# Masked attention with LayerNorm on one core: transposes and broadcast one slot later, the finish behind the mask, and work moved from VectorE to ScalarE and GpSimd

## The reference, cut to what matters

```python
scores = einsum('nd,md->nm', x, ks)                      # 8192 x 8192, d = 128, float32
scores = leaky_relu(scores, negative_slope=0.2)
scores = where(adj > 0, scores, NEG_BIG)                 # adj: int32, 8192 x 8192
attn = softmax(scores, axis=1)
y = x + einsum('nm,md->nd', attn, ks)
out = (y - mean(y)) / sqrt(var(y) + 1e-5)                # LayerNorm over d
```

## Time and profile before

| | us |
|---|---|
| median of three runs (1758.53 to 1759.35) | 1758.76 |
| the profiled execution's own time | 1757.06 |
| its span, first to last instruction | 1755.0 |
| TensorE matmul busy | 1554.2 (89%) |
| VectorE busy | 1547.7 (88%) |
| ScalarE busy | 1441.9 (82%) |
| GpSimd busy | 1408.3 (80%) |

### The profile page before, as it was taken

How to read it: one execution, slowest core, us unless ns; L and a number is a source line. 1 busy time by engine, 2 the same in 40 slices (tenths; PEclk the granted TensorE clock), 3 DMA queues, 4 the chain that set the end, 5 groups by cost and what they waited for, 6 DMA issues and landing times. The chain is left out here.

```text
span 1755.0 us, 42403 instructions
## 1 busy us (share of the span) xinstructions
PE 1554.2 (89%) x16576; PEld 1446.4 (82%) x16576; DVE 1547.7 (88%) x1855; ACT 1441.9 (82%) x1810; POOL 1408.3 (80%) x1167
## 2 busy tenths in 40 slices
PE   2689999999999999999999999999999999999985
PEld 1488888988888988888988888888888888888885
DVE  7998989998999989899989998999898999989971
ACT  4588878888888988888989887888887888888885
POOL 0488878888888978788978887988887888878898
PEclk9899999999999999999999999999999999999999
DMA  9654445554544444445445445444444544444510
GB/s 356 232 194 151 170 159 175 178 172 159 176 163 179 166 171 173 159 171 178 168 163 178 161 171 175 174 155 175 170 164 173 175 164 169 174 164 164 176 55 7
DMA packets 67799, 296.34 MB, mean 169 GB/s; under 512 B 6160, under 2 KB 32784, under 8 KB 34832
## 3 DMA queue, kind: packets, MB, share of 16 engines
q1 hardware_dynamic: 67600, 293.63, 47.4%
HBM read 289.41 MB, written 4.19 MB: 167 GB/s over the span
## 5 line engine op out<-in xcount | busy, mean ns | idle before, releaser
L280 POOL TENSOR_TENSOR ring<-ring,floor 128x768 f32<-128x768 f32 (+1 forms) x512 | 797.5, 1558 | 100.9 <-ACT floor L374 100.9
L351 ACT ACTIVATE scores<-scores,shrink 128x1024 f32<-128x1024 f32 x512 | 553.2, 1081 | 267.3 <-PE scores L579 264.4
L479 DVE SCALAR_TENSOR_TENSOR ring<-adj_sb,scores 128x1024 f32<-128x1024 int32 x512 | 622.1, 1215 | 144.7 <-ACT scores L351 142.0
L611 PE MATMUL weighted<-k_rows,ring 128*128 128x129 f32 x4096 | 547.8, 277 | 74.3 <-DVE y L534 74.3
L577 PE MATMUL scores<-xt_hi,kt_hi 128*128 128x256 f16 x2048 | 566.1, 276 | 48.0 <-DVE xt_lo L444 29.8
L284 POOL TENSOR_TENSOR pt_lo<-ring,pt_hi 128x512 f16<-128x512 f32 x512 | 594.4, 1162 | 13.1 <-ACT pt_hi L363 13.1
L492 DVE TENSOR_TENSOR running<-ring,running 128x1024 f32<-128x1024 f32 x480 | 585.6, 1220 | 0.0
L357 ACT ACTIVATE ring<-ring,lift 128x1024 f32<-128x1024 f32 x512 | 583.9, 1140 | 1.3 <-DVE ring L513 0.7
L611 PEld LDWEIGHTS weighted<-k_rows,ring 128*128 128x128 f32 x4096 | 501.0, 192 | 87.1 <-issue 80.5
L579 PE MATMUL scores<-xt_hi,kt_lo 128*128 128x256 f16 x2048 | 566.5, 277 | 0.0
L578 PE MATMUL scores<-xt_lo,kt_hi 128*128 128x256 f16 x2048 | 566.2, 276 | 0.0
(11 more groups left out here) (50 smaller groups left out, 409.6 us busy)
## 6 DMA issues: line engine op xcount, KB each, us to landing
adj_sb<-in_adj SPq DMA_DIRECT2D x256, 1024.0 KB, 4.9
ring<-in_ks_t SPq DMA_DIRECT2D x8, 512.0 KB, 6.8
ring<-in_x_t SPq DMA_DIRECT2D x8, 512.0 KB, 13.1
xt_raw<-in_x_t SPq DMA_DIRECT2D x32, 128.0 KB, 4.8
x_row<-in_x SPq DMA_DIRECT2D x32, 128.0 KB, 4.9
out<-normed SPq DMA_DIRECT2D x32, 128.0 KB, 5.2
k_rows<-in_ks SPq DMA_DIRECT2D x16, 128.0 KB, 3.1
ring<-in_ks SPq DMA_DIRECT2D x1, 2048.0 KB, 9.3
```

Source lines behind the costliest of these rows:

```text
L280: nc.gpsimd.tensor_tensor(here, here, below, ALU.subtract).then_inc(gap_ready, 1)
L479: nc.vector.scalar_tensor_tensor(ring[:, g % RING, :, :], adj_sb[:, n % ADJS, half * QUAD:(half + 1) * QUAD, :], 0.0, scores[:, g % 2, :, ...
L611: nc.tensor.matmul(weighted[:, j * LANES:(j + 1) * LANES], ring[:, g % RING, t, j * P:(j + 1) * P], k_rows[:, q, t, 0:LANES], start=(q == ...
```

## The change

- `turn` is at delay 18 and stands, on TensorE, behind the scores of its slot and ahead of `weigh` (before: delay 17, at the slot's end). `spread` is at delay 19, and `lowest` stays at 17.
- `finish` is at delay 38 and stands on VectorE behind the slot's mask (before: 39, at the slot's head). `mean`, `squares_of`, `deviation`, `normalise` and the store follow one slot earlier, too. `mean` and `deviation` stand at the end of GpSimd's slot, and `low_part` ahead of `gap`.
- The copy of a block's first group into `running` is on ScalarE (`first`, delay 2, behind `bend`).
- The low parts of x and of four eighths of the keys are made on GpSimd, each by two instructions (scale in place, subtract) in place of one.
- In the last 16 groups VectorE takes three tiles of the `gap` and GpSimd one.
- VectorE's gap waits for the copy `floor` of its own block at all groups, and the first masks no longer wait for the keys' low parts, but for those whose ring places still hold the raw keys (8 to 15).

```diff
-    AT_TURN, AT_SPREAD = 17, 18
-    AT_FINISH = LAST + AT_WEIGH + 1
+    AT_LOWEST, AT_TURN, AT_SPREAD = 17, 18, 19
+    AT_FIRST = 2
+    AT_FINISH = LAST + AT_WEIGH
...
-            return 1 + g % 2
+            return 3 if g >= ALL - GROUPS else 1 + g % 2
...
+            def split_x(b):
+                pool.wait_ge(xt_hi_ready, b + 1)
+                wait(pool, scores_ready, GROUPS * (b - 1))
+                here = xt_raw[:, b % 2, :]
+                nc.gpsimd.tensor_scalar(here, here, scale_x, 1.0, ALU.mult, ALU.mult).then_inc(xt_scaled_ready, 1)
+                pool.wait_ge(xt_scaled_ready, b)
+                pool.wait_ge(xt_lo_ready, b)
+                nc.gpsimd.tensor_tensor(xt_lo[:, b % 2, :], here, xt_hi[:, b % 2, :], ALU.subtract)\
+                    .then_inc(xt_lo_ready, 1)
...
+            for c in range(EARLY, STEPS):
+                low_ks_t(c)
+            split_x(1)
             part_rows()
             for s in SLOTS:
+                g = group(s, AT_PART)
+                if g is not None:
+                    low_part(g)
+                g = group(s, AT_GAP)
+                if g is not None:
+                    gap(g)
                 b = whole(s, AT_FINISH + 1)
                 if b is not None:
                     mean(b)
                 b = whole(s, AT_FINISH + 2)
                 if b is not None:
                     deviation(b)
-                g = group(s, AT_GAP)
-                if g is not None:
-                    gap(g)
-                g = group(s, AT_PART)
-                if g is not None:
-                    low_part(g)
+                b = whole(s, -5)
+                if b is not None and b > 1:
+                    split_x(b)
...
+            def first(g):
+                act.wait_ge(masked_ready, g + 1)
+                wait(act, low_ready, g // GROUPS)
+                wait(act, running_ready, g)
+                nc.scalar.activation(running[:, :, :], ring[:, g % RING, :, :], ACT.Copy).then_inc(running_ready, 1)
...
-                if g < RING:
-                    dve.wait_ge(kt_lo_ready, min(STEPS, max(1, g - 7)))
+                if 8 <= g < 16:
+                    dve.wait_ge(kt_lo_ready, g - 7)
...
-            for c in range(EARLY, STEPS):
-                split_ks_t(c)
             for s in SLOTS:
+                g = group(s, 0)
+                if g is not None:
+                    mask(g)
                 b = whole(s, AT_FINISH)
                 if b is not None:
                     finish(b)
-                g = group(s, 0)
-                if g is not None:
-                    mask(g)
-                b = whole(s, AT_SPREAD - 1)
+                b = whole(s, AT_LOWEST)
                 if b is not None:
                     lowest(b)
```

More of the change, by code:

```diff
@@ L139, in adj_attention_layernorm @@
         kt_lo_ready = sem("kt_lo_ready")
+        kt_scaled_ready = sem("kt_scaled_ready")
         xt_hi_ready = sem("xt_hi_ready")
+        xt_scaled_ready = sem("xt_scaled_ready")
         xt_lo_ready = sem("xt_lo_ready")
@@ L257, in _, with low_ks_t @@
                                                bass.bass_isa.ReduceOp.max).then_inc(mag_all_ready, 1)
+            def low_ks_t(c):
+                cols = slice(c * STEP, (c + 1) * STEP)
+                pool.wait_ge(kt_hi_ready, c + 1)
+                nc.gpsimd.tensor_scalar(ks_t_raw[:, cols], ks_t_raw[:, cols], scale_k, 1.0, ALU.mult, ALU.mult)\
+                    .then_inc(kt_scaled_ready, 1)
+                pool.wait_ge(kt_scaled_ready, c - EARLY + 1)
+                pool.wait_ge(kt_lo_ready, c)
+                nc.gpsimd.tensor_tensor(kt_lo[:, cols], ks_t_raw[:, cols], kt_hi[:, cols], ALU.subtract)\
+                    .then_inc(kt_lo_ready, 1)
+            def split_x(b):
[7 more added lines that the diff above has]
+                    .then_inc(xt_lo_ready, 1)
             def part_rows():
@@ L411, in _ @@
                     spread(b)
+                b = whole(s, AT_FIRST)
+                if b is not None:
+                    first(b * GROUPS)
                 b = whole(s, -6)
-                if b is not None and b > 0:
+                if b is not None and b > 1:
                     split_x(b)
@@ L486, in least @@
                 here = ring[:, g % RING, :, :]
-                if g % GROUPS == 0:
-                    wait(dve, low_ready, g // GROUPS)
-                    nc.vector.tensor_copy(running[:, :, :], here).then_inc(running_ready, 1)
-                else:
-                    dve.wait_ge(running_ready, g)
-                    nc.vector.tensor_tensor(running[:, :, :], here, running[:, :, :], ALU.min)\
-                        .then_inc(running_ready, 1)
+                dve.wait_ge(running_ready, g)
+                nc.vector.tensor_tensor(running[:, :, :], here, running[:, :, :], ALU.min).then_inc(running_ready, 1)
             def columns(b):
@@ L501, in gap @@
             def gap(g):
-                b, j = divmod(g, GROUPS)
+                b = g // GROUPS
                 tiles = dve_tiles(g)
-                dve.wait_ge(spread_ready, b + 1)
-                if j == LAST and b + 1 < BLOCKS:
-                    dve.wait_ge(floor_ready, b + 2)
-                else:
-                    dve.wait_ge(floor_ready, b + 1)
+                dve.wait_ge(floor_ready, b + 1)
                 dve.wait_ge(running_ready, g + 1)
@@ L553, in _ @@
                 g = group(s, 1)
-                if g is not None:
+                if g is not None and g % GROUPS:
                     least(g)
@@ L557, in _ @@
                         columns(g // GROUPS)
-                b = whole(s, -5)
-                if b is not None and b > 0:
-                    split_x(b)
         @block.tensor
@@ L593, in spread @@
                 wait(pe, floor_ready, b)
-                wait(pe, dve_gap_ready, GROUPS * b - 1)
+                wait(pe, dve_gap_ready, GROUPS * b)
                 for j in range(SIDES):
@@ L634, in _ @@
                     score(g)
+                b = whole(s, AT_TURN)
+                if b is not None:
+                    turn(b)
                 b = whole(s, AT_SPREAD)
@@ L640, in _ @@
                     weigh(g)
-                b = whole(s, AT_TURN)
-                if b is not None:
-                    turn(b)
 def kernel(x, adj, L0_gnn_ks):
```

## The result

| | before | after |
|---|---|---|
| median of the runs, us | 1759.05 | 1672.61 (1671.93 to 1675.17) |
| ratio to before, 95% interval | | 0.951 (0.9493 to 0.9526) |
| the profiled execution, its span | 1757.06, 1755.0 | 1672.36, 1670.1 |
| mean granted clock | 0.985 | 0.997 |
| from the first to the last weighing of a block in the steady part (29 blocks) | 52.3 us a block | 50.06 us a block |

The account below looks back on a forecast made before the run. A chain through GpSimd, ScalarE and VectorE was taken to bound a block at 50.1 us. Savings of 63.7 + 4.0 + 2.1 + 10.0 = 79.8 us gave a forecast of 1679 us, 8 in 10 within 1643 to 1714.

Parts of the forecast that it names:

- TensorE's waits: At transposes 1.69 falls to 0.4 us, for the finish 2.43 to 0.8; by these and the spread, a block takes 48.6.
- The spread's 0.3: TensorE's spread waits some 0.3 us for VectorE's lowest and the gap behind it; this was to go.
- the third wait: A new TensorE wait of 1.5 us a block, about four slots behind the finish, for VectorE's mask of slot 41.
- The chain: One turn through GpSimd, ScalarE and VectorE takes 50.1 us, longer than TensorE's 48.6, and so sets the block.
- five stretches: GpSimd to the mean 12.4, squares to deviation 5.3, normalise to mask 3.4, VectorE to column minimum 22.1, to GpSimd's gap 6.9.
- The falls of the clock: TensorE's clock drops to half behind the finish's wait, costing 0.46 us a block; all of it was counted as gained.
- The sum: Savings of 63.7 us in 29.5 blocks, 4.0 and 2.1 at the start and 10.0 in the drain: 79.8 us.
- The start: First two blocks save 2.0 us each in waits, and the second block's low part of x leaving VectorE saves 2.1.
- The tiles: In the drain GpSimd takes one gap tile in place of three or two, saving 12.5 us.
- the two idle times on GpSimd: In the drain, hand-overs of slots 40 and 41 leave GpSimd idle about 1.6 us each, costing 3.2 us.
- The other edits: Taking the copy (1.1 us) and x (0.6 us) a block off VectorE adds nothing of its own, since VectorE pauses anyway.
- GpSimd's own price for x: The low part of x as two GpSimd operations in slot 43: 1.1 us at the most, at least 0.2.

Follow-up runs that it names:

- run 1: The changed kernel with squares and deviation at slot 41 and normalise at slot 43, the store two slots later: 1618.35 us.
- Run 9: The changed kernel with one tile of the gap of each block's first group (slot 35) moved from GpSimd to VectorE: 1669.74 us.
- run 5: The changed kernel with the copy of a block's first group back on VectorE: 1704.23 us.
- run 8: The changed kernel with transposes and spread back in their old places on TensorE, with the two gap waits belonging to them: 1708.19 us.
- run 2: The changed kernel with one extra ScalarE copy of 512 columns a block, right behind normalise in slot 41: 1689.44 us.
- run 10: The changed kernel with GpSimd's order alone changed: mean ahead of the gap in slot 39, deviation ahead of low part and gap in slot 40: 1614.47 us.
- run 6: The changed kernel with the low part of x, from the third block on, back on VectorE: 1705.32 us.
- run 4: The changed kernel with the finish back at delay 39, ahead of the mask, and mean, squares, deviation, normalise and store one slot later: 1782.55 us.
- run 12: The edits of run 1 and run 4 together, on the changed kernel: 1704.17 us.
- run 7: The changed kernel with VectorE taking one or two gap tiles in the last block again, GpSimd three or two: 1685.37 us.

## Why the prediction was right

*TensorE's waits.* Forecast 0.4 at the transposes and 0.8 for the finish, measured 0.32 and 0.70 each block. The spread's 0.3 was said to go and stayed (0.28): the gap that it waits for moved a slot later with it. This step failed, by 0.3 us a block. The time in brackets was also taken for the whole price of a wait, which it is not (run 1): TensorE's path without the third wait was forecast at 48.6 us and is 48.33 with no wait at the transposes either.

*The chain, and the third wait.* All five stretches are within 0.33 us of their forecasts, the errors (-0.15 to +0.33) cancel by luck to less than 0.1, the block is 50.06 against 50.1, and the wait stands where it was forecast, 1.03 us against 1.5. What failed is the reading "the sum is 50.1 us, longer than TensorE's 48.6, so a block lasts 50.1 us". The number held, and for the cause only the last 0.12 us of it: TensorE's own path is not 48.6 but 49.94 us long, since the third wait is part of its own path. Run 9 shortened the chain by 0.52 us and the block by 0.12; in runs 5 and 8, where GpSimd waits in slot 39 and the chain is open, the block grew by 1.0 with TensorE's waits. That the two lengths lie 0.12 us apart, so that one number served for both, was luck. What remains of the step is what both ways share: the hand-overs between GpSimd and ScalarE in slots 40 and 41 (runs 1, 2 and 10, worth 1.7 to 1.9 us a block), and VectorE's stretch from the mask of slot 41 to the column minimum, in which 0.94 us more lengthened the block by 1.05 (run 6).

*The falls of the clock.* None in 28 blocks, as forecast; the waits left are 0.28 to 1.03 us. The Trainium skill (TensorE: Matmul & The Clock Gate, section "What's actually happening"), by which the array's busyness over a time decides and short pauses could add up, is neither shown nor refuted. In run 4, with waits of 2.42 and 1.09 us in a block, the clock fell in 20 blocks and in run 12, with 2.43 and no second wait of that size, in 15; but in the kernel before, with 2.43 and 1.69, it fell in 9 only. So a second pause does not order them.

*The sum.* Between the first wait for a finish and the thirtieth the blocks saved 29 x 2.29 = 66.3 us, forecast 63.7. The start was mis-sized: the first finish comes at 136.48 in place of 147.16, 10.7 us sooner, of which I had 6.1. I had taken the waits of later blocks there (2.0 us for each of two blocks, though by the sum above it 1.6 go). In the kernel before VectorE pauses for only 3.6 us between 66 and 147 us, so nearly each microsecond taken off it could count; that fits the trace, but was not tried by itself. From the thirtieth wait to the end it is 7.9 us, forecast 10.0. The tiles were priced at 12.5 us (run 7: 12.8), and the two idle times on GpSimd are there as expected (1.66 and 1.51 us); GpSimd's own drain is 42.3 - 32.6 = 9.7 us shorter, and not all of that reaches the end. That is 84.9 us of the span and 84.7 of the profiled time, where 79.8 were forecast; the errors (+4.6, +2.6 and -2.1) cancel in part.

*The other edits.* "They add nothing of their own" was wrong for both. The copy (run 5, 32 us) and the low part of x (run 6, 33 us) are each worth about 1 us a block in this kernel: the one stands ahead of the gap that TensorE's spread waits for, the other in front of the transposes. I had looked for pauses of VectorE in the kernel before, and not for what it is late for in the kernel after. In the forecast this is hidden, since I added up the stretches without both. GpSimd's own price for x, 0.56 and 0.63 us from start to start, 1.2 in all, was forecast 1.1. The Trainium skill (GPSIMD Engine Reference, section 4.1) calls GpSimd about twice as slow as VectorE for operations with two inputs, by which the subtraction is an estimated 1.3 us against VectorE's 0.66. The trace does not agree: it took 0.67 us. VectorE's 0.66 had waiting in it, however; with GpSimd idle, at the start, VectorE took 0.48 us.

*The parts do not add up.* Put back singly into the changed kernel, finish, transposes, copy and x cost 110, 36, 32 and 33 us, 210 together, and the whole change won 86. Each part removed one wait, and the new wait of slot 41 (54 to 58 us by runs 1 and 10) had to be paid from it; that makes some 140 to 144 of the 210. Of the rest, the falls of the clock that run 4 has over the kernel before (20 against 9 of 28 blocks, 1.64 us each) are an estimated 20 us. What makes up the remaining 45 or so was not tried.

## What to carry to other kernels

When steps that feed one another across two engines are moved a slot nearer, look at what stands ahead of each in its own queue, not only at its slot number: here a gap ahead of the mean (an instruction of 0.2 us), and a low part and a gap ahead of the deviation, cost 1.9 us in every block (50.06 against 48.19, run 10). A chain whose sum equals the measured period can have a second one close behind it, and then little is won by shortening it; shorten one stretch of it that nothing else uses, and see how far the period follows. And an edit is priced against the kernel with the other edits in it, where the next wait stands close behind.

## What the runs showed of the hardware

- The idle time in a matmul's brackets is less than what the wait costs. Score matmuls are listed with 0.27 us each and start 0.11 us apart. The third wait shows 1.03 us and costs 1.18 from start to start, that at the transposes shows 0.32 and costs 0.52 (the changed kernel against run 1).
- Whether the clock falls behind one and the same wait of 2.43 us changes from block to block and from kernel to kernel (9, 15 and 20 of 28). It is not without order: in run 12 it fell in nearly every second block, in run 4 mostly in three of four. The cause stays open. A fall costs 1.64 us in run 12 (52.00 against 50.36). Behind waits up to 1.7 us none was seen in the steady blocks of any of the kernels.
- What VectorE's subtraction of 256 columns takes, with all its tensors in SBUF, is set by GpSimd. It took 0.48 us at the start with GpSimd idle, 0.66 before, 1.01 in run 6 and 2.20 beside a long GpSimd instruction, the same instruction each time. In 30 of the 31 others in the kernel before and in all 30 others of run 6 it ended 0.28 us behind the end of the GpSimd instruction that was running when it started; that at 64.29 us, for one, ends at 66.49, and GpSimd's, of 7.66 us, at 66.20. GpSimd's next instruction was longer by 0.2 us (a gap 2.02 in place of 1.82 before, a low part 1.34 in place of 1.16 in run 6). VectorE's masks, which read PSUM, took 1.21 to 1.22 us beside it.
